# A fused four-layer graph network on one core: GpSimd's work for the first block is put off, the first block's loop over row tiles is reordered, and a small first layer is computed on 96 partitions

## The chip, the cores and the metric

The kernel runs on one core of one Trainium2 chip. The time is the device time of one execution in microseconds (us); before the change it was 3078.63 us, the median of 3 runs (3078.52 to 3081.78).

## What is computed

Four graph layers in a row on 1250 nodes with 512 features and 20000 edges, each added to `x` after a layer norm and a ReLU. The first layer holds nearly all that the change touches:

```python
h = maximum(layernorm(x), 0)
emb  = concat([sin(noise * freqs), cos(noise * freqs)])          # 1250 x 64
cond = silu(emb @ f_w1 + f_b1) @ f_w2 + f_b2                     # 64 -> 16 -> 16
for i in range(4):                                               # four blocks
    y = xhat(h) * (1 + cond @ s1_w[i] + s1_b[i]) + cond @ b1_w[i] + b1_b[i]
    q, k, v = y @ wq[i] + bq[i], y @ wk[i] + bk[i], y @ wv[i] + bv[i]
    att = softmax over the edges that leave each node, 4 heads of 128
    h = h + att_sum(v) @ wo[i] + bo[i]
    y = xhat(h) * (1 + cond @ s2_w[i] + s2_b[i]) + cond @ b2_w[i] + b2_b[i]
    h = h + relu(y @ m_w1[i] + m_b1[i]) @ m_w2[i] + m_b2[i]
x = x + h
# then a mean over neighbours, a gated relational layer and a two-step mean layer
```

`xhat` is the normalised row. The sums over edges are done with dense 1250 x 1250 matrices of edge counts. The mean of the last layer divides by the number of edges that enter each node.

## The kernel before

There is no scheduler: each engine has its own program, in the order in which it is written, and the engines wait for each other by semaphores. Nodes lie as 10 row tiles of 125 (T = 10, P = 125), or transposed on 128 partitions (`yT`).

**Head of the program.** SyncE (SP) loads the edge lists, the conditioning's small weights `fw1`, `fw2`, `fb1`, `fb2` and then `x`, all with no wait (L485 to L490). Semaphore `pre_in` counts the small weights and `x`; VectorE waits for it before it makes the phases (`first_phases`, L806). GpSimd fills constants, and signals `consts_set`, for which VectorE's first operation waits.

**Placement of edges.** 160 steps (EC = 160) follow. In each, GpSimd writes one `row_hot`, VectorE two `slot_hot`, and TensorE multiplies them (L1584) into one PSUM tile. Other work is woven in by step number: the statistics of `x`; at step 10 the first conditioning layer (L1591) with ScalarE's bias and exponential (L1315, L1317); at step 25 VectorE's end of the SiLU (`finish_silu`, L838 to L845: add one, reciprocal, product), on 16 partitions x 1250 elements; at 30, 35 and 40 the second layer (L1596); from 46 on the first norm.

**After the steps.** VectorE makes `placef`, `placei` and the constants `ident_r` (L940 to L963), and then, group by group (59 groups), one-hot matrices from which TensorE builds the counts (L1608, L1615) and ScalarE copies them (L1345, L1348). GpSimd, after its last `row_hot`, goes on at once to block 0: `stack_matrices(1)` (L663 and twice L666, the matrices of the second norm, from `stage`, which shares `oT`), and the bias of the output row, added to all of `x` in one instruction (L690). Both are wanted much later: the first (`cw_ready`) by ScalarE's first `copy_o`, which overwrites `oT`, and by the second norm; the second (`xbias_done`) by VectorE at head 1.

**The loop over row tiles in block 0.** The counts are needed transposed. For each row tile t, TensorE transposes 10 pieces of 125 x 125 (`turn_counts`, L1628) into one PSUM tile, ScalarE copies that to one of three buffers (`copy_turned`, two instructions at L1357), SP writes the buffer to HBM (`crow_d`, L522), VectorE makes a mask from it (`mask_row`, L990), TensorE makes the scores (`max_scores`, L1704), and VectorE takes their masked maximum in two halves (`masked_max`, L1014). `turn_counts(t + 1)` stands ahead of `max_scores(t)` on TensorE, and may write only after ScalarE has copied row tile t. After row tiles 2, 4, 6 and 8 (`TAKE_AT`) TensorE makes one part of head 1's projections (8 matmul records at L1636), which ScalarE takes to `qk_hi` (`high_part`, L1371) and VectorE to `qk_lo` (`low_part`, L1005). ScalarE also sums each row tile of `ct` into `per_in` (L1403, with a throw-away output `junk` in `pacc`). ScalarE's order in it is:

```python
for t in range(T):
    copy_turned(t)
    A.activation(junk, ct[:, t, :], ACT.Copy, accum_out=per_in[:, t:t + 1])
    A.drain()
    if t in TAKE_AT:
        high_part(1, TAKE_AT.index(t))
```

After the loop come the negated maxima (L1020, L1022), `max_row(0)` (L1742), two more parts of projections, and the heads. Each block ends with a two-layer perceptron; its first product is the `up` loop: 12 jobs of 8 matmul records at L1636, each taken over by ScalarE with ReLU (L1434), in two PSUM slots.

## Time and profile before

| what | value |
|---|---|
| median of 3 runs | 3078.63 us (3078.52 to 3081.78) |
| the profiled execution, its own time | 3081.62 us |
| its span, first to last instruction | 3079.9 us |
| TensorE busy | 2855.9 us, 93% |
| VectorE busy | 2052.6 us, 67% |
| ScalarE busy | 866.2 us, 28% |
| GpSimd busy | 714.1 us, 23% |
| mean granted TensorE clock | 0.969 |
| chain that ended last, by engine | PE 73%, DVE 17%, issue 4%, ACT 3% |

PE is TensorE's matmul queue, PEld its weight loads, DVE VectorE, ACT ScalarE, POOL GpSimd. A name with q (ACTq, SPq) is that engine's sequencer. The chain follows the execution back from the last instruction, at each step to what released it. The stages that matter here, in us of the span: placement steps 41 to 200, the constants after them 199 to 220, groups 220 to 388, block 0's first projections 388 to 409, its loop over row tiles 409 to 460, its heads from 472, its `up` loop 787 to 816.

### The profile page before, as it was taken

The page shows a single profiled execution, that of the slowest core. Times are in us where ns is not written, and L with a number is a line of the kernel's source. Part 1 is how long each engine was busy: PE and PEld are TensorE (multiplying, and loading weights), DVE is VectorE, ACT ScalarE, POOL GpSimd, SP SyncE. Part 2 cuts the span into 40 slices and gives each one's busy share as a digit, 9 for nine tenths or more (in the row PEclk, how much of TensorE's full clock was granted, in tenths as well). Part 3 has the DMA queues.
Part 4 walks back from the last instruction along what each step waited for, and adds up shares of the span by engine and source line. Part 5 has one row for each costly group of instructions (what it writes and reads, how often), then busy time and mean ns, then how long its engine had stood idle before and what let it go on. Part 6 is the DMA issues. An engine that isn't in the chain of part 4 may idle for free.

```text
span 3079.9 us, 31253 instructions
## 1 busy us (share of the span) xinstructions
PE 2855.9 (93%) x11230; PEld 1816.5 (59%) x11230; DVE 2052.6 (67%) x3758; ACT 866.2 (28%) x1154; POOL 714.1 (23%) x639
## 2 busy tenths in 40 slices
PE   2869979999999999999999999999999999999999
PEld 0336646676556666555667555667645566556555
DVE  8889946776757776766777674778686876623211
ACT  2218842222212222221222321222322213213221
POOL 3760003333023334031334120334320000000000
PEclk9989989999999999999999999999999999999999
DMA  4000020000400000320000230000145244421001
GB/s 106 1 1 1 1 89 7 1 28 14 126 35 14 1 28 14 97 64 14 1 28 1 66 109 14 1 15 14 47 127 166 65 128 142 130 80 40 14 1 34
DMA packets 74678, 143.61 MB, mean 47 GB/s; under 512 B 11428, under 2 KB 11819, under 8 KB 74524
## 3 DMA queue, kind: packets, MB, share of 16 engines
q1 hardware_dynamic: 68988, 129.58, 13.7%
q0 software_dynamic: 5536, 12.03, 1.2%
q8 instruction: 90, 1.47, 0.2%
q14 instruction: 64, 0.52, 0.1%
HBM read 130.66 MB, written 10.92 MB: 46 GB/s over the span
## 4 chain that ended last, share of the span: by engine, by line
PE 73%; DVE 17%; issue 4%; ACT 3%; DMA 1%; DVEq 1%; POOL 1%; ACTq 0%; SPq 0%
PE ps L1636 13%; PE ps L1859 11%; PE ps L1888 10%; PE ps L1730 6%; PE ps L1833 4%; PE ps L1545 4%; PE ps L1608 4%; DVE prob L1069 4%; DVE x L1059 3%; PE ps L1562 2%; PE ps L1880 2%; PE ps L1719 2%; DVE ps L1014 2%; PE ps L1704 2%; PE ps L1721 2%
## 5 line engine op out<-in xcount | busy, mean ns | idle before, releaser
L706 POOL TENSOR_TENSOR pacc<-pacc,prob 125x628 f32<-125x628 f32 (+1 forms) x288 | 404.7, 1405 | 350.6 <-DVE prob L1088 350.6
L1636 PE MATMUL ps<-yT,w 128*128 128x416 f32 (+1 forms) x1152 | 442.2, 541 | 15.2 <-DVE qk_lo L1005 5.9
L1730 PE MATMUL ps<-prob,big 125*128 125x314 f32 x1280 | 394.8, 431 | 14.0 <-DVE prob L1088 10.9
L1417 ACT ACTIVATE prob<-prob 125x628 f32<-125x628 f32 x320 | 233.0, 728 | 574.7 <-DVE prob L1069 574.7
L1888 PE MATMUL ps<-pieces,counts_r 125*125 125x512 f32 x1400 | 353.3, 406 | 0.0
L1636 PEld LDWEIGHTS ps<-yT,w 128*128 128x128 f32 x1152 | 229.3, 201 | 202.8 <-issue 188.9
L1088 DVE SCALAR_TENSOR_TENSOR prob<-prob,typed 125x628 f32<-125x628 f32 x320 | 260.1, 813 | 70.3 <-ACT prob L1417 68.1
L1888 PEld LDWEIGHTS ps<-pieces,counts_r 125*125 125x125 f32 x1400 | 257.2, 185 | 76.9 <-issue 17.4
L1719 PE MATMUL ps<-qk_hi 128*125 128x314 f32 x640 | 271.5, 424 | 11.2 <-DVE prob L1069 10.6
L1730 PEld LDWEIGHTS ps<-prob,big 125*128 125x128 f32 x1280 | 228.0, 190 | 81.3 <-DVE prob L1088 27.2
L1014 DVE CUSTOM_DVE_ANT_0 ps<-ps,typed 125x628 f32<-125x628 f32 x320 | 257.9, 816 | 10.0 <-PE ps L1704 9.9
L1069 DVE TENSOR_TENSOR prob<-ps,shift 125x628 f32<-125x628 f32 x320 | 257.4, 804 | 6.2 <-PE ps L1721 5.6
L1005 DVE SCALAR_TENSOR_TENSOR qk_lo<-ps,bcol,qk_hi 128x416 fp32r<-128x416 f32 (+1 forms) x96 | 62.3, 651 | 261.5 <-ACT qk_hi L1371 261.5
L702 POOL TENSOR_TENSOR pacc<-prob,zcol 125x628 f32<-125x628 f32 (+1 forms) x32 | 39.3, 1228 | 751.6 <-DVE prob L1088 751.6
L1720 PE MATMUL ps<-qk_lo,qk_hi 128*125 128x314 f32 x640 | 197.9, 309 | 0.0
L1721 PE MATMUL ps<-qk_hi,qk_lo 128*125 128x314 f32 x640 | 197.9, 309 | 0.0
L643 POOL TENSOR_TENSOR rstd<-var,mhalf 125x1 f32<-125x1 f32 x110 | 71.8, 652 | 535.9 <-DVE var L867 535.9
L1115 DVE SCALAR_TENSOR_TENSOR lite_acc<-lite_ring,att_w,lite_acc 128x512 f32<-128x512 f32 x232 | 180.7, 820 | 10.9 <-DMA lite_ring<-in_basis 1.9
L1169 DVE SCALAR_TENSOR_TENSOR w<-basis,att_w,w 128x512 f32<-128x512 f32 x232 | 167.3, 748 | 22.8 <-DMA basis<-in_basis 10.0
L1778 PE MATMUL ps<-w,oT 128*125 128x512 f32 x320 | 180.1, 648 | 1.5 <-DVE x L1059 1.5
L1719 PEld LDWEIGHTS ps<-qk_hi 128*125 128x125 f32 x640 | 120.0, 188 | 103.3 <-DVE prob L1069 82.5
L1371 ACT ACTIVATE qk_hi<-ps,bcol 128x416 fp32r<-128x416 f32 (+1 forms) x96 | 58.1, 609 | 396.6 <-PE ps L1636 396.6
(214 smaller groups left out, 4488.2 us busy)
## 6 DMA issues: line engine op xcount, KB each, us to landing
basis<-in_basis SPq DMA_DIRECT2D x160, 256.0 KB, 2.7
lite_ring<-in_basis SPq DMA_DIRECT2D x120, 256.0 KB, 2.6
w<-in_m_w SPq DMA_DIRECT2D x8, 1024.0 KB, 6.6
w<-in_wk SPq DMA_DIRECT2D x5, 1024.0 KB, 6.4
w<-in_wv SPq DMA_DIRECT2D x4, 1024.0 KB, 5.5
oT<-in_cw SPq DMA_DIRECT2D x8, 512.0 KB, 4.1
w<-in_wq SPq DMA_DIRECT2D x4, 1024.0 KB, 5.4
w<-in_wo SPq DMA_DIRECT2D x4, 1024.0 KB, 5.4
```

Of the source, the lines that this page charges most:

```text
L706: nc.gpsimd.tensor_tensor(pacc[:, c0:c0 + nn], pacc[:, c0:c0 + nn], prob[:, n % 3, p0:p0 + nn], ALU.add).then_inc(psum_done, 1)
L1014: V.tensor_tensor_reduce(out=score_ps(s.slot), in0=score_ps(s.slot), in1=in_quarters(mneg[:, t, c0:c0 + HALF]), scale=1.0, scalar=-BIG, op ...
L1069: V.tensor_tensor(in_quarters(prob[:, n % 3, :]), score_ps(s.slot), in_quarters(shift[:, c0:c0 + HALF]), ALU.add).then_inc(shifted, 1)
L1088: V.scalar_tensor_tensor(out=prob[:, n % 3, 0:nn], in0=prob[:, n % 3, 0:nn], scalar=BIG, in1=ct[:, t, c0:c0 + nn], op0=ALU.min, op1=ALU.mu ...
L1417: A.activation(prob[:, n % 3, :], prob[:, n % 3, :], ACT.Exp, scale=DH ** -0.5).then_inc(exp_done, 1)
L1636: last = mm(lin_ps(job, 128, nn), weight[:, k, m * 128:(m + 1) * 128], lhs[:, k, c0:c0 + nn], start=(k == 0), stop=(k == KD - 1))
L1719: mm(o, hi[:, 1, rows], hi[:, 0, cols], start=True, stop=False)
L1720: mm(o, hi[:, 1, rows], lo[:, 0, cols], start=False, stop=False)
L1721: last = mm(o, lo[:, 1, rows], hi[:, 0, cols], start=False, stop=True)
L1730: last = mm(o_halves[:, b, :], vrow[:, t, h * DH:(h + 1) * DH], prob[:, n % 3, b * QUARTER:(b + 1) * QUARTER], start=(t == 0), stop=(t == ...
L1859: last = mm(post_ps(job, P, D), lhs[:, k, t * P:(t + 1) * P], weight[:, k, :], start=(k == 0), stop=(k == KD - 1))
L1888: last = mm(post_ps(job, P, D), counts_r[:, slot, k, :], pieces[:, piece, k, :], start=(self_ is None and k == 0 and piece == 0), stop=(k ...
```

## The change

1. **GpSimd** in block 0 waits for `mneg_ready` 1 (the mask of row tile 0) ahead of `stack_matrices(1)`, and adds the bias one row tile at a time, piece t after mask t: ten instructions of 512 elements in place of one of 5120.
2. **The loop** takes each part of head 1's projections one row tile later on ScalarE and VectorE (`t - 1 in TAKE_AT`). TensorE's order is as before.
3. **The sums** `per_in` go from ScalarE's loop to the `up` loop of block 0, one after each of its first ten jobs, with `junk` in `shift`. VectorE's maximum and reciprocal of them go to block 1.
4. **Conditioning**: the first layer's product writes 96 partitions from a weight with three copies of `f_w1` at columns 0, 32 and 64; ScalarE takes from each of the three column ranges of 418 its own 32 partitions, so that `z`, `zexp` and `silu` are 96 x 418 in place of 16 x 1250. SP loads `fw1`, `fw2` and `fb1` three times, after `consts_set`; GpSimd clears `fw1` and `fb1` ahead of it.

```diff
...
         ident16 = sk("ident16", [P, P], F16)
-        fw1 = sk("fw1", [2 * FREQS, COND], F32)
-        fw2 = sk("fw2", [COND, 128], F32)
-        fb1 = sk("fb1", [COND, 1], F32)
+        fw2 = sk("fw2", [96, 128], F32)
+        fb1 = sk("fb1", [96, 1], F32)
         fb2 = sk("fb2", [128, 1], F32)
...
         emb = yT[0:2 * FREQS, 3, :]
-        z = hidT[0:COND, 0, :]
-        zexp = hidT[0:COND, 1, :]
-        silu = hidT[0:COND, 2, :]
+        z = hidT[0:96, 0, 0:418]
+        zexp = hidT[0:96, 1, 0:418]
+        silu = hidT[0:96, 2, 0:418]
 
...
         egr = sa("egr", [128, BUCKETS], F32)
+        fw1 = sa("fw1", [2 * FREQS, 96], F32)
         gcmp = sa("gcmp", [128, GROUPS + 1, BUCKETS], F32)
...
         skip_x_last = prob[:].rearrange("p s n -> p (s n)")[:, 2 * D:3 * D]
-        junk = pacc[:].bitcast(F16)[:, 0:N]
         cw = sl("cw", [128, 4, D], F32R)
...
         shift = sl("shift", [P, N], F32)
+        junk = shift[:].bitcast(F16)[:, 0:N]
         bias_r = sl("bias_r", [P, D], F32R)
...
             sp.dma_start(noise, a["node_vec1"].partition_broadcast(2 * FREQS)).then_inc(phase_ready, 16)
-            for dst_, name in ((fw1, "L0_gnn_f_w1"), (fw2, "fw2_stack"), (fb1, "f_b1"), (fb2, "fb2_stack")):
-                sp.dma_start(dst_[:], a[name]).then_inc(pre_in, 16)
+            sp.wait_ge(consts_set, 1)
+            for k in range(3):
+                for dst_, name in ((fw1[:, 32 * k:32 * k + COND], "L0_gnn_f_w1"), (fw2[32 * k:32 * k + COND, :], "fw2_stack"),
+                                   (fb1[32 * k:32 * k + COND, :], "f_b1")):
+                    sp.dma_start(dst_, a[name]).then_inc(pre_in, 16)
+            sp.dma_start(fb2[:], a["fb2_stack"]).then_inc(pre_in, 16)
             sp.dma_start(x[:], a["x"].rearrange("(t p) d -> p t d", p=P)).then_inc(pre_in, 16)
...
             nc.gpsimd.memset(ident[:], 0.0)
+            nc.gpsimd.memset(fw1[:], 0.0)
+            nc.gpsimd.memset(fb1[:], 0.0)
             nc.gpsimd.memset(ident16[:], 0.0)
...
                     if half == 0:
+                        if i == 0:
+                            pool.wait_ge(mneg_ready, 1)
                         stack_matrices(1, at(i, 32, 32))
...
                     pool.wait_ge(blkc_in, at(i, 32, 32))
-                    nc.gpsimd.tensor_tensor(x[:], x[:], brow[:, 1:2, :].to_broadcast([P, T, D]),
-                                            ALU.add).then_inc(xbias_done, 1)
+                    if i:
+                        nc.gpsimd.tensor_tensor(x[:], x[:], brow[:, 1:2, :].to_broadcast([P, T, D]),
+                                                ALU.add).then_inc(xbias_done, 1)
+                    else:
+                        for t in range(T):
+                            pool.wait_ge(mneg_ready, t + 1)
+                            last = nc.gpsimd.tensor_tensor(x[:, t, :], x[:, t, :], brow[:, 1, :], ALU.add)
+                        last.then_inc(xbias_done, 1)
                     for h in range(HEADS):
...
                 dve.wait_ge(phase_ready, 16)
-                dve.wait_ge(pre_in, 80)
+                dve.wait_ge(pre_in, 176)
                 V.tensor_scalar(turns, noise, freq[:], 1.0 / 16.0, ALU.mult, ALU.mult)
...
                     masked_max(0, 2 * t + 1)
-                    if i == 0 and t in TAKE_AT:
-                        low_part(1, TAKE_AT.index(t))
+                    if i == 0 and t - 1 in TAKE_AT:
+                        low_part(1, TAKE_AT.index(t - 1))
                 negate_max(0)
...
                 if i == 0:
-                    dve.wait_ge(edges_counted, 2)
                     V.tensor_tensor(per_out, per_out, edges_out[:, :, 1], ALU.add)
-                    V.tensor_scalar(per_in[:], per_in[:], 1.0, None, ALU.max)
                     V.drain()
                     V.reciprocal(per_out, per_out)
+                if i == 1:
+                    dve.wait_ge(edges_counted, T)
+                    V.tensor_scalar(per_in[:], per_in[:], 1.0, None, ALU.max)
+                    V.drain()
                     V.reciprocal(per_in[:], per_in[:])
...
             A.activation(cw[:, 0:2, :], stage, ACT.Copy).then_inc(cw_hi, 1)
-            for (c0, nn), job in zip(COLS, hj):
+            for k, job in enumerate(hj):
+                rows = slice(32 * k, 32 * k + 32)
                 act.wait_ge(lin_full, job.full)
-                A.activation(z[:, c0:c0 + nn], lin_ps(job, COND, nn), ACT.Identity, bias=fb1[:]).then_inc(lin_empty[job.slot], 1)
+                A.activation(z[rows, :], lin_ps(job, 96, 418)[rows, :], ACT.Identity, bias=fb1[rows, :]).then_inc(lin_empty[job.slot], 1)
             A.drain()
...
                         copy_turned(t)
-                        A.activation(junk, ct[:, t, :], ACT.Copy, accum_out=per_in[:, t:t + 1])
-                        A.drain()
-                        if t in TAKE_AT:
-                            high_part(1, TAKE_AT.index(t))
-                    A.drain().then_inc(edges_counted, 2)
+                        if t - 1 in TAKE_AT:
+                            high_part(1, TAKE_AT.index(t - 1))
                 else:
...
                                  bias=bcol[:, 2, k:k + 1]).then_inc(lin_empty[job.slot], 1)
+                    if i == 0 and n < T:
+                        A.activation(junk, ct[:, n, :], ACT.Copy, accum_out=per_in[:, n:n + 1])
+                        A.drain().then_inc(edges_counted, 1)
                     if n == 5 and i + 1 < BLOCKS:
...
                 if c == HIDDEN_AT:
-                    pe.wait_ge(pre_in, 80)
+                    pe.wait_ge(pre_in, 176)
                     pe.wait_ge(emb_ready, 2)
-                    for (c0, nn), job in zip(COLS, hj):
+                    for k, job in enumerate(hj):
                         reuse(job)
-                        mm(lin_ps(job, COND, nn), fw1[:], emb[:, c0:c0 + nn], start=True, stop=True).then_inc(lin_full, 1)
+                        mm(lin_ps(job, 96, 418), fw1[:], emb[:, 416 * k:416 * k + 418], start=True, stop=True).then_inc(lin_full, 1)
                 if c in COND_AT:
                     pe.wait_ge(silu_ready, 1)
-                    (c0, nn), job = COLS[COND_AT.index(c)], cj[COND_AT.index(c)]
+                    k = COND_AT.index(c)
+                    (c0, nn), job, rows = COLS[k], cj[k], slice(32 * k, 32 * k + COND)
                     reuse(job)
-                    mm(lin_ps(job, 128, nn), fw2[:], silu[:, c0:c0 + nn], start=True, stop=True).then_inc(lin_full, 1)
+                    mm(lin_ps(job, 128, nn), fw2[rows, :], silu[rows, c0 - 416 * k:c0 - 416 * k + nn],
+                       start=True, stop=True).then_inc(lin_full, 1)
                 n, rest = divmod(c - NORM_AT, NORM_EVERY)
```

GpSimd's program from the last `row_hot` to block 0's first sum of probabilities, before and then now:

```order
L648 TENSOR_SCALAR row_hot<-col_iota,slot_row 125x128 x38
L663 TENSOR_TENSOR cw<-oT,zcol 128x1024
L666 TENSOR_TENSOR cw<-oT,cw 32x1024 x2
L690 TENSOR_TENSOR x<-x,brow 125x5120
L702 TENSOR_TENSOR pacc<-prob,zcol 125x628
```

```order
L654 TENSOR_SCALAR row_hot<-col_iota,slot_row 125x128 x38
L669 TENSOR_TENSOR cw<-oT,zcol 128x1024
L672 TENSOR_TENSOR cw<-oT,cw 32x1024 x2
L704 TENSOR_TENSOR x<-x,brow 125x512 x10
L716 TENSOR_TENSOR pacc<-prob,zcol 125x628
```

The order of the instructions stays; the new wait stands between the first row and the second, and the one bias instruction has become ten.

ScalarE in block 0's loop, from the second half of row tile 2's copy on (`prob` is the buffer of the transposed counts, `typed` is `ct`), before and then now:

```order
L1357 ACTIVATE prob,edges_out<-ps 125x250
L1403 ACTIVATE pacc,per_in<-typed 125x1250
L1371 ACTIVATE qk_hi<-ps,bcol 128x418
L1357 ACTIVATE prob,edges_out<-ps 125x1000
L1357 ACTIVATE prob,edges_out<-ps 125x250
L1403 ACTIVATE pacc,per_in<-typed 125x1250
L1357 ACTIVATE prob,edges_out<-ps 125x1000
L1357 ACTIVATE prob,edges_out<-ps 125x250
L1403 ACTIVATE pacc,per_in<-typed 125x1250
L1371 ACTIVATE qk_hi<-ps,bcol 128x416
L1357 ACTIVATE prob,edges_out<-ps 125x1000
```

```order
L1374 ACTIVATE prob,edges_out<-ps 125x250
L1374 ACTIVATE prob,edges_out<-ps 125x1000
L1374 ACTIVATE prob,edges_out<-ps 125x250
L1388 ACTIVATE qk_hi<-ps,bcol 128x418
L1374 ACTIVATE prob,edges_out<-ps 125x1000
L1374 ACTIVATE prob,edges_out<-ps 125x250
L1374 ACTIVATE prob,edges_out<-ps 125x1000
L1374 ACTIVATE prob,edges_out<-ps 125x250
L1388 ACTIVATE qk_hi<-ps,bcol 128x416
L1374 ACTIVATE prob,edges_out<-ps 125x1000
```

The sums are gone from between the copies, and the part whose product follows row tile 4 (the second `qk_hi` row) is taken after the copy of row tile 5, no longer ahead of it.

## Rows read from the trace of the kernel before

**Rows 1.** The profile's page, busy time of the engines

```profile
PE 2855.9 (93%) x11230; PEld 1816.5 (59%) x11230; DVE 2052.6 (67%) x3758; ACT 866.2 (28%) x1154; POOL 714.1 (23%) x639
```

**Rows 2.** Timeline of VectorE, 66 to 79 us (start, length, engine, line, operation, idle before)

```profile
67.70 0.79 DVE L840 TENSOR_SCALAR big<-big 16x1250 f32<-16x1250 f32 x1
68.57 7.95 DVE L842 RECIPROCAL big<-big 16x1250 f32<-16x1250 f32 x1
76.59 1.45 DVE L844 TENSOR_TENSOR big<-big 16x1250 f32<-16x1250 f32 x1
```

**Rows 3.** Timeline of TensorE, 66 to 110 us

```profile
78.91 2.71 PE L1584 MATMUL ps<-slot_hot,row_hot 125*128 125x472 f16 x5 [10.43 <-DVE slot_hot L923]
```

**Rows 4.** Timeline of VectorE, 199 to 220 us

```profile
202.46 0.25 DVE L945 TENSOR_SCALAR bk<-bk 128x60 f32<-128x60 f32 x1
...
202.91 2.33 DVE L948 TENSOR_SCALAR placef<-bk 128x59 f32<-128x59 f32 x1
...
205.61 2.18 DVE L953 CAST placei<-placef 128x59 int32<-128x59 f32 x1
...
208.90 10.19 DVE L961 CAST ident_r<-ident 125x125 fp32r<-125x125 f32 x1
```

**Rows 5.** Timeline of GpSimd, 199 to 220 us

```profile
199.38 3.27 POOL L663 TENSOR_TENSOR cw<-oT,zcol 128x1024 fp32r<-128x1024 f32 x1 [0.16 <-issue]
202.79 4.94 POOL L666 TENSOR_TENSOR cw<-oT,cw 32x1024 fp32r<-32x1024 f32 x2
208.05 10.96 POOL L690 TENSOR_TENSOR x<-x,brow 125x5120 f32<-125x5120 f32 x1 [0.31 <-issue]
```

**Rows 6.** Timeline of TensorE, 176 to 232 us

```profile
220.85 5.92 PE L1608 MATMUL ps<-onehot_src,onehot_dst 128*125 128x512 f16 x24 [20.76 <-DVE onehot_src L979]
```

**Rows 7.** Timeline of ScalarE, 386 to 500 us

```profile
423.50 1.00 ACT L1357 ACTIVATE prob<-ps 125x1000 f16<-125x1000 f16 x1 [2.10 <-DMA crow_d<-prob]
...
434.08 0.61 ACT L1371 ACTIVATE qk_hi<-ps,bcol 128x416 fp32r<-128x416 f32 x1 [5.08 <-PE ps L1636]
```

**Rows 8.** Chain that ended last, 425 to 460 us (start, length, what)

```profile
441.39 3.33 PE ps L1636 x8
...
444.99 1.26 ACTq L1404
...
446.70 1.23 ACT pacc L1403 x2
...
449.57 1.33 PE ps L1628 x10
450.90 1.15 PE ps L1704 x4
...
457.20 0.49 DVE typed L990
...
457.82 0.82 DVE ps L1014
```

**Rows 9.** Timeline of TensorE, 432 to 472 us

```profile
436.09 0.80 PE L1628 MATMUL ps<-ident,typed 125*125 125x125 f16 x10 [2.04 <-ACT prob L1357]
436.69 0.82 PE L1704 MATMUL ps<-qk_hi 128*125 128x314 f32 x4
...
460.07 2.46 PE L1742 MATMUL ps<-ident_r,nmx 125*125 125x126 f32 x10 [4.32 <-DVEq L1023]
462.68 7.59 PE L1636 MATMUL ps<-yT,w 128*128 128x416 f32 x16 [0.16 <-ACT shift L1382]
```

**Rows 10.** Windows by 4 us (length; PE, PEld, DVE, ACT, POOL busy; PEclk, DMA share, GB/s)

```profile
460.00:464.00 4.00, 3.77 (x12) 3.09 (x13) 0.00 (x0) 1.49 (x3) 0.00 (x0) 0.50 0.72 240
```

**Rows 11.** Windows by 1 us, the load of x and of the first weights

```profile
32.00:33.00 1.00, 0.00 (x0) 0.00 (x0) 1.00 (x1) 0.00 (x0) 0.00 (x0) 1.00 0.01 4
```

**Rows 12.** Timeline of the SP queue, 0 to 42 us

```profile
4.74 0.33 SPq L490 DMA_DIRECT2D x<-in_x  x1
```

**Rows 13.** Groups of TensorE, 786 to 817 us (busy, mean ns; idle before)

```profile
L1636 PE MATMUL ps<-yT,w 128*128 128x416 f32 (+1 forms) x80 | 28.2, 513 | 1.3 <-ACT big L1434 1.3
```

2 lines of the change are left out of this document (1 added, 1 removed).

## The prediction, made blind

> **What bounds the kernel now.** I read the page first. TensorE is busy 93% of the span [rows 1], so only its gaps, and matmuls that ran at the lower of its two clocks, can be won, and those lie mostly in the first 480 us. I then followed the chain that ended last through that part and read each engine's timeline where the chain leaves TensorE. There are three such places.
>
> First, VectorE's end of the SiLU takes 0.79, 7.95 and 1.45 us [rows 2], of which the reciprocal is nearly all. TensorE stands idle for 10.43 us and goes on when VectorE has made the next `slot_hot` [rows 3].
>
> Second, after the placement steps a small cast to int32 takes 2.18 us, and the cast of a 125 x 125 tile 10.19 us, where an operation of the same kind on 60 elements takes 0.25 [rows 4]. GpSimd's instructions explain it: `placef` begins at 202.91, just after GpSimd's `cw` instruction at 202.79, and ends at 205.24, the middle of the two that make up 4.94 us; `placei` ends at 207.79, and the pair at 207.73; the cast of `ident` ends at 219.09, and GpSimd's addition to `x` at 219.01 [rows 4, 5]. Three times VectorE is let go when a GpSimd instruction ends. TensorE waits 20.76 us in all here [rows 6].
>
> Third, block 0's loop over row tiles. ScalarE first waits for a transfer of `crow_d`, until 423.50 [rows 7]. From then on a pair of row tiles takes 10.66 us (441.39 to 452.05, the end of row 450.90). In it the chain goes from TensorE's product (3.33) to ScalarE, which has waited for the product (5.08 us idle [rows 7]) and only then copies a row tile (1.26 and what follows), sums (1.23), copies the next, and then back to TensorE's transposes (1.33) and scores (1.15) [rows 8].
>
> **The change, term by term.**
>
> *SiLU.* The three operations go from 1250 to 418 elements in a partition, 832 fewer. A fixed part of 0.15 us each taken off, an element costs 6.24 ns in the reciprocal, 0.51 and 1.04 in the others [rows 2]. That is 5.19 + 0.43 + 0.87 = **6.5 us**, all on VectorE and in TensorE's gap of 10.43 us [rows 3]. No row shows these operations on 96 partitions. The mask, with the same 1250 elements (of two bytes) on 125 partitions, takes 0.49 us [rows 8] where 16 partitions took 0.79, so the time goes by elements in a partition; the other bound, nothing won, I leave to the range's upper part with the loads. GpSimd is ahead at that point. The matmuls, with 96 output partitions in place of 16, stay as many and as wide.
>
> *Loads.* SP now waits for `consts_set`, some 5 us into the span, and issues six more small loads. `x` was issued at 4.74 [rows 12]; with those issues of 0.45 to 0.65 us each I put it at about 10.7, 5.9 us later. The queue was quiet by 32.0 [rows 11], with the first weights behind `x` in it, so `x` lands by about 35 to 37. VectorE asks for it at 36.2. I cost this at nothing; what hides it is the head's long VectorE operations, and each us beyond costs one. Bound: 3 us. GpSimd's two more memsets come before VectorE's first input is there.
>
> *GpSimd put off.* `placef` falls by 2.08, `placei` by 1.93 to 1.98 and the cast of `ident`, with 125 elements, by about 9.95 [rows 4]: **14.0 us** at the start of the groups, which no other engine holds: TensorE waits for VectorE alone there [rows 6]. Bounds 13.5 and, if TensorE also starts at a better clock after a shorter rest, 15.
>
> Where does the work go? In the loop, mask 0 ends at about 409.8 and GpSimd then runs 3.27 + 4.94 us [rows 5] to 418.2, and the pieces for row tiles 0, 1 and 2, some 1.1 to 1.3 us each (10.96 for ten [rows 5]), to about 422. Masks 1 and 2 may wait up to 1.2 us for an instruction of GpSimd's to end, but nothing is late before ScalarE's wait for the transfer ends at 423.50 [rows 7]. That wait is the cover. After it each piece begins when its mask is written and the next mask comes 2.7 us or more later. So I cost it at 0; without the cover it would be 8.2 us for the matrices. Queued behind the new wait on GpSimd are only these and the sums of probabilities, wanted at 474.
>
> The Trainium skill (SBUF — State Buffer, section "Who interferes with whom") says that a VectorE instruction in a 2-port mode and a GpSimd instruction exclude each other for the whole length of whichever came first. The trace agrees three times over, as above. It also speaks against the new place, since the mask is of such a kind; by it the cost could be as the second rival says.
>
> *The loop.* ScalarE no longer holds row tile 5, 7 or 9 back for the product, and doesn't sum. The cycle of a pair becomes TensorE's: product, transposes, copy, transposes, scores. At full clock that is 2.82 (28.2 us for 80 records, 8 to a product [rows 13]) + 0.80 [rows 9] + 1.55 (a copy: two instructions of which the first takes 1.00 [rows 7], with its gaps) + 0.80 + 0.82 [rows 9] = 6.8 us. At the clock of this trace's slower records it is 3.33 + 0.80 + 1.55 + 1.33 + 1.15 = 8.2 [rows 8]. TensorE now rests less than the 2.04 us of before [rows 9], after which it was still fast, so I take 7.3. The product after row tile 4 ends at about 434.1, when ScalarE takes it [rows 7]. Two more pairs end at 448.7; then come the scores of row tile 9, two maxima of 0.82 [rows 8], the part taken later (0.65) and the negation: `max_row` at about 452.0, where it was at 460.07 [rows 9]. **8.1 us**, with bounds 5 and 9.5. The transfers of `crow_d` don't bind: ScalarE waited for one of ten.
>
> *Behind it.* `max_row` and the 16 records of projection ran 2.46 and 7.59 us [rows 9], at half clock at first [rows 10]; 16 records at full clock take 5.6 [rows 13]. TensorE's rest ahead of them falls from 4.32 us [rows 9] to about 2.6. I take **1.0 us** of the 2.2, and **0.2** for two small operations on VectorE that leave. Bounds 0 and 2.4.
>
> *Sums in the `up` loop.* Ten times some 1.5 us (the chain's 1.23 and the accumulator's read [rows 8]) beside 0.6 of ReLU make 2.2 us of ScalarE in a product's 2.82 [rows 13]. Hidden under TensorE, cost 0; at most 1.6 us, at the job where ScalarE also converts the next block's matrices.
>
> Sum: 6.5 + 14.0 + 8.1 + 1.0 + 0.2 = 29.8 us. The profiled execution took 3081.6, so it would take 3051.8; it was 3.0 above the median of the runs. Against the median of 3078.63 I predict **3048.8 us**.
>
> **Rivals.** (1) *The loop hardly gains* (0.14): TensorE stays at its slower clock, or each `crow_d` transfer takes as long as the first did (over 14 us from its issue at about 409.2), and ScalarE waits again. For it: the first wait exists. Against: no second one does. The other terms are left, 20.5 us: 3058.1. (2) *GpSimd's work lands on the loop* (0.05): masks wait for it and the transfer's wait doesn't cover. The matrices cost 8.2 us and each of seven later masks up to 1.1: 15.9 us back, 3064.7. Against: the times above. (3) *The long casts are not GpSimd's doing* (0.04): then 14.0 us stay, 3062.8. Against it are three ends within 0.1 us of each other. (4) *Slower* (0.02): ScalarE's sums throttle the `up` loop. Its two PSUM slots empty only when ScalarE is through, so the loop's pace becomes ScalarE's as soon as a sum takes over 2.2 us (2.82 less 0.6); ten of 5.2 us each would give back all 29.8, and ten of 6 us 37.8, which makes 3086.6. The row of 1.23 us speaks against it. (5) *`x` comes late* (0.05), by more than 3 us: at 5 us, 3053.8.
>
> **How the numbers follow.** The forecast has 0.70. All its low ends (3.5 for SiLU and loads, 13.5, 5, 0) make 22.0 us, 3056.6; its high ones (6.5, 15, 9.5, 2.4) make 33.4, 3045.2. The range reaches to rival 1 above and 1 us beyond below, for the scatter of the median: 3044.2 to 3058.5. What a measurement of this kernel can tell from no change is about 0.2%, 6.2 us. All cases but the fourth are faster by more than that: faster 0.96, same 0.02 (several of the ends together), slower 0.02.
>
> **What would show it.** Right: a reciprocal of 2.7 to 2.8 us on 96 partitions and TensorE's gap there near 4; the cast of `ident` below 0.4 us, and the first group's matmul some 20.5 us earlier (200.3); GpSimd's `cw` instructions after mask 0 and over before ScalarE's wait for the transfer ends; a pair of row tiles of 7 to 8 us; no wait of TensorE for ScalarE in the `up` loop of block 0 beyond the 1.3 us of now [rows 13]. Wrong: a wait of VectorE at 36 us for `x`; more than one wait for `crow_d`; masks that take over 1 us behind the first three; a total that differs from the sum of these places, which would mean that a stage further on had used the gap.

## The result, and the profile after

| what | before | changed |
|---|---|---|
| median | 3078.57 us (3076.79 to 3081.78, 4 runs) | 3041.79 us (3041.54 to 3042.7, 4 runs) |
| ratio | | 0.988, 95% interval 0.9863 to 0.9897 |
| profiled execution, span | 3081.62 us, 3079.9 us | 3042.7 us, 3041.0 us |
| PE, DVE, ACT, POOL busy | 2855.9, 2052.6, 866.2, 714.1 us | 2845.3, 2034.2, 865.5, 714.3 us |
| mean granted TensorE clock | 0.969 | 0.975 |

The kernel is 36.8 us faster. The forecast was 29.8, and the median lies 2.4 us below the low end of its range. Two later sets of runs gave 35.3 and 32.8 us (3078.49 to 3043.16, 3076.5 to 3043.72): the median of before moved between 3076.5 and 3079.9 from set to set, that of the changed kernel between 3041.8 and 3043.7. So the forecast was short by 3 to 7 us.

The page's first rows after, to [rows 1]:

```profile
span 3041.0 us, 31271 instructions
...
PE 2845.3 (94%) x11230; PEld 1808.7 (59%) x11230; DVE 2034.2 (67%) x3758; ACT 865.5 (28%) x1154; POOL 714.3 (23%) x650
```

**Start.** Timeline of VectorE, 35 to 71 us (start, length, engine, line, operation, shapes; idle time before in brackets), to [rows 2]:

```profile
35.76 0.93 DVE L823 TENSOR_SCALAR yT<-yT,freq 64x1250 f32<-64x1250 f32 x1
...
67.37 0.36 DVE L854 TENSOR_SCALAR big<-big 96x418 f32<-96x418 f32 x1
67.81 2.76 DVE L856 RECIPROCAL big<-big 96x418 f32<-96x418 f32 x1
70.64 0.59 DVE L858 TENSOR_TENSOR big<-big 96x418 f32<-96x418 f32 x1
```

The reciprocal takes 2.76 us (7.95 before), the other two 0.36 and 0.59 (0.79 and 1.45). At 35.76 no wait stands before VectorE's first operation that needs the loads behind `x`'s place in the queue, and none came later: the loads cost nothing. TensorE's gap there, to [rows 3]:

```profile
72.10 2.71 PE L1601 MATMUL ps<-slot_hot,row_hot 125*128 125x472 f16 x5 [3.95 <-DVE slot_hot L937]
```

3.95 us in place of 10.43. **Constants.** VectorE from 196 to 198 us, to [rows 4], and TensorE at the start of the groups, to [rows 6]:

```profile
196.04 0.18 DVE L962 TENSOR_SCALAR placef<-bk 128x59 f32<-128x59 f32 x1
...
196.60 0.19 DVE L967 CAST placei<-placef 128x59 int32<-128x59 f32 x1
...
197.91 0.23 DVE L975 CAST ident_r<-ident 125x125 fp32r<-125x125 f32 x1
```

```profile
199.89 6.49 PE L1627 MATMUL ps<-onehot_src,onehot_dst 128*125 128x512 f16 x20 [6.62 <-DVE onehot_src L993]
```

The cast of `ident` takes 0.23 us where it took 10.19, TensorE's idle time is 6.62 where it was 20.76, and the first group's matmul starts at 199.89 (220.85 before; 200.3 was forecast). **Where GpSimd's work went.** Timelines of GpSimd and of VectorE's masks, 390 to 404 us, to [rows 5]:

```profile
390.35 1.89 POOL L669 TENSOR_TENSOR cw<-oT,zcol 128x1024 fp32r<-128x1024 f32 x1 [197.94 <-DVE typed L1004]
392.38 4.91 POOL L672 TENSOR_TENSOR cw<-oT,cw 32x1024 fp32r<-32x1024 f32 x2
397.62 3.71 POOL L704 TENSOR_TENSOR x<-x,brow 125x512 f32<-125x512 f32 x3 [0.33 <-issue]
403.99 1.28 POOL L704 TENSOR_TENSOR x<-x,brow 125x512 f32<-125x512 f32 x1 [2.66 <-DVE typed L1004]
```

```profile
389.77 0.49 DVE L1004 TENSOR_SCALAR typed<-prob 125x1250 bf16<-125x1250 f16 x1 [0.56 <-issue]
...
392.47 2.61 DVE L1004 TENSOR_SCALAR typed<-prob 125x1250 bf16<-125x1250 f16 x1
...
396.72 0.92 DVE L1004 TENSOR_SCALAR typed<-prob 125x1250 bf16<-125x1250 f16 x1
...
403.42 0.49 DVE L1004 TENSOR_SCALAR typed<-prob 125x1250 bf16<-125x1250 f16 x1 [4.01 <-ACT prob L1374]
```

Mask 1 is held for 2.1 us (its instruction is recorded as 2.61 us long where a free one takes 0.49), mask 2 for 0.4, later ones not at all; and ScalarE still waits before the fourth row tile, 7.52 us here, so this costs nothing at mask 3. **The loop.** A pair is two row tiles, from one product of TensorE (L1655) to the next. Chain that ended last, 413 to 426 us (start, length, what), to [rows 8], and TensorE's `max_row`, to [rows 9]:

```profile
413.84 2.79 PE ps L1655 x8
416.63 0.60 PE ps L1647 x10
...
418.15 0.56 ACT prob L1374 x3
418.72 0.04 issue
418.76 0.79 PE ps L1647 x10
419.55 0.63 PE ps L1723 x4
420.18 2.81 PE ps L1655 x8
```

```profile
426.06 1.09 PE L1761 MATMUL ps<-ident_r,nmx 125*125 125x126 f32 x8 [2.50 <-DVEq L1037]
...
427.86 7.22 PE L1655 MATMUL ps<-yT,w 128*128 128x416 f32 x16
```

ScalarE stands in the chain only with the copy (416.63 + 0.60 to 418.76), the product and its sum are gone from it, and a pair of row tiles takes 6.34 us (413.84 to 420.18) in place of 10.66. `max_row` is 34.0 us earlier than before.

**Where the gain is.** Two profiles of before and three of the changed kernel (the first, and those of r1_before, r2_after and r4_after below) give, as means:

| stretch | before | changed | gain | forecast |
|---|---|---|---|---|
| start to mask 0 | 409.90 | 389.94 | 20.0 | 20.5 |
| mask 0 to `max_row` | 48.80 | 36.95 | 11.8 | 8.1 |
| `max_row` to the first exponential | 13.49 | 11.76 | 1.7 | 1.2 |
| first exponential to the end of the span | 2605.8 | 2602.6 | 3.2 | 0 |

### The profile page after: what moved, and what is told of

It reads as the page before. It is cut to its first block, busy times and chain, and to the rows that moved or that the text cites. A ratio compares the mean times of both kernels' runs of the same rounds, so it can differ in the third digit from the quotient of the medians.

```text
span 3041.0 us, 31271 instructions
## 1 busy us (share of the span) xinstructions
PE 2845.3 (94%) x11230; PEld 1808.7 (59%) x11230; DVE 2034.2 (67%) x3758; ACT 865.5 (28%) x1154; POOL 714.3 (23%) x650
## 4 chain that ended last, share of the span: by engine, by line
PE 73%; DVE 16%; issue 4%; ACT 3%; DMA 1%; DVEq 1%; POOL 1%; SPq 0%; ACTq 0%
PE ps L1655 13%; PE ps L1878 11%; PE ps L1907 10%; PE ps L1749 6%; PE ps L1852 5%; PE ps L1562 5%; PE ps L1627 4%; DVE prob L1085 4%; DVE x L1075 3%; PE ps L1579 2%; PE ps L1899 2%; PE ps L1738 2%; DVE ps L1028 2%; PE ps L1723 2%; ACT prob L1431 2%
## 5 line engine op out<-in xcount | busy, mean ns | idle before, releaser
L1655 PE MATMUL ps<-yT,w 128*128 128x416 f32 (+1 forms) x1152 | 440.8, 540 | 15.0 <-DVE qk_lo L1019 5.9
L1655 PEld LDWEIGHTS ps<-yT,w 128*128 128x128 f32 x1152 | 228.7, 201 | 201.3 <-issue 187.7
L1738 PE MATMUL ps<-qk_hi 128*125 128x314 f32 x640 | 271.7, 424 | 11.6 <-DVE prob L1085 11.3
L1131 DVE SCALAR_TENSOR_TENSOR lite_acc<-lite_ring,att_w,lite_acc 128x512 f32<-128x512 f32 x232 | 180.4, 819 | 11.5 <-DMA lite_ring<-in_basis 1.9
L1723 PE MATMUL ps<-qk_hi 128*125 128x314 f32 x640 | 152.9, 330 | 7.8 <-issue 6.8
```

The lines of the kernel that those rows point to most:

```text
L1655: last = mm(lin_ps(job, 128, nn), weight[:, k, m * 128:(m + 1) * 128], lhs[:, k, c0:c0 + nn], start=(k == 0), stop=(k == KD - 1))
L1723: last = mm(score_ps(s.slot)[:, b, :], qk_hi[:, h % 2, 0, t * P:(t + 1) * P], qk_hi[:, h % 2, 1, c0:c0 + QUARTER], start=True, stop=True)
L1738: mm(o, hi[:, 1, rows], hi[:, 0, cols], start=True, stop=False)
```

## The experiments

All are timed against the kernel before, which ran again in each set of runs; a ratio is taken to before in the same set, with its 95% interval, and a gain to the set's median of before. The table has, for each profile, the stretch from mask 0 to mask 3 (it holds ScalarE's wait for the `crow_d` transfer), and that from mask 3 to `max_row`, worked out from the starts of VectorE's masks and of TensorE's `max_row`.

| kernel | median us | mask 0 to 3 | mask 3 to `max_row` | sum |
|---|---|---|---|---|
| before, first profile | 3078.57 | 15.69 | 35.08 | 50.77 |
| r1_before: again | 3078.14 | 14.32 | 32.51 | 46.83 |
| e1_cond96: before + 96 partitions | 3073.33 | 14.30 | 34.15 | 48.45 |
| e2_pool: before + GpSimd's put-off | 3062.30 | 15.39 | 34.95 | 50.34 |
| e4_sums: before + sums moved | 3076.81 | 13.25 | 34.24 | 47.49 |
| e13_split_before: before + stores in two | 3077.50 | 11.71 | 35.48 | 47.19 |
| e3_order: before + order | 3065.02 | 13.78 | 26.03 | 39.81 |
| e5_loop: before + order + sums | 3066.30 | 14.92 | 25.69 | 40.61 |
| changed, first profile | 3041.79 | 13.65 | 22.64 | 36.29 |
| r2_after: again | 3043.16 | 13.73 | 24.75 | 38.48 |
| r4_after: again | 3043.72 | 13.48 | 22.61 | 36.09 |
| e10_sums_back: changed, sums in the loop | 3047.11 | 14.85 | 25.51 | 40.36 |
| e6_no_pool: changed, GpSimd as before | 3057.65 | 13.87 | 24.33 | 38.20 |
| e9_fill: e6_no_pool + a product twice | 3060.07 | 15.37 | 25.00 | 40.37 |
| e7_pool5: changed, matrices at mask 4 | 3046.00 | 13.55 | 25.70 | 39.25 |
| e12_early: changed, matrices at the groups' end | 3045.19 | 15.08 | 24.99 | 40.07 |
| e8_split: changed, stores in two | 3038.71 | 9.50 | 24.54 | 34.04 |
| e14_early_sums_back: e11 with sums in the loop | 3042.14 | 9.08 | 24.61 | 33.69 |
| e11_split_early: e8 + e12 | 3036.89 | 7.37 | 23.66 | 31.03 |
| r3_best: e11 again | 3036.23 | 8.15 | 23.69 | 31.84 |

### The four parts one by one

**e1_cond96.** The hunks of the diff on `fw1`, `fb1`, `fw2`, `z` and their loads, and nothing else.

> The kernel before with the conditioning's first layer on 96 partitions and nothing else (loads, matmuls, SiLU). Theory: the reciprocal falls from 7.95 us to 2.8, the other two of VectorE by 1.3 in all, and all of it reaches the end: the last placement step, the groups and block 0 stand 6.3 to 6.8 us earlier, and the time is 3072 us. Rival: the placement steps behind the SiLU are held by GpSimd's or TensorE's pace and take it back: VectorE's first copy of a typed bucket stands less than 3 us earlier, time 3076 to 3079. Second rival: what is won at 70 us depends on the other parts.

3073.33 us, ratio 0.9981 (0.9972 to 0.9991): 6.6 us less than the set's 3079.91, by the interval 2.8 to 8.6. The reciprocal took 2.76 us. In the trace mask 0 stands 5.3 us and the first exponential 7.3 us earlier. The term holds by itself.

**e2_pool.** The two hunks on GpSimd alone: `pool.wait_ge(mneg_ready, 1)`, and ten pieces of the bias.

> The kernel before with GpSimd's put-off alone (matrices wait for mask 0, the bias addition in ten pieces), the loop and the sums as before. Theory: the casts to placei and of ident fall to about 0.25 us, 14 us at the start of the groups, 1.2 of it given back by the first group's matmuls at the lower clock; the loop stays at its old pace (a pair of row tiles 10.66 us) because its order is the old one; time 3065.5. Rival A: the put-off work is what made the new loop fast beyond the forecast (shorter wait for the crow_d transfer, TensorE at the upper clock after it): then mask 3 follows mask 0 by 13.7 us and not 15.7, and a pair takes under 10 us; time about 3060. Rival B: in the old loop GpSimd's pieces hold masks back and a pair takes over 11 us; time above 3068.

3062.3 us, ratio 0.9946 (0.9929 to 0.9962), 17.6 us less than the set's before. In the trace mask 0 is 13.5 us earlier and the first exponential 13.6; the other 4 stand behind the first exponential (2600.8 us against 2606.9), where the edit touches nothing. The loop took 50.34 us, in the range of kernels with its order, and mask 3 followed mask 0 by 15.4. Pairs took 9.1 to 11.6 us, as they did in r1_before (9.1 to 11.5) with no work of GpSimd beside them: rival A is out, and so is B.

**e3_order.** On the kernel before:

```diff
-                    if i == 0 and t in TAKE_AT:
-                        low_part(1, TAKE_AT.index(t))
+                    if i == 0 and t - 1 in TAKE_AT:
+                        low_part(1, TAKE_AT.index(t - 1))
```

and the same for ScalarE's `high_part`, the sum left ahead of it.

> The kernel before with ScalarE and VectorE taking each product of the loop one row tile later, the sums left in the loop, GpSimd's work and the SiLU as before. Theory (the order lets TensorE go on, and TensorE that rests less keeps the upper clock): transposes at 0.80 and scores at 0.82 us behind the first wait, a pair of row tiles at ScalarE's own pace, 2 x (1.55 copy + 1.45 sum) + 0.65 product and gaps = about 7.0 us against 10.66; max_row about 10 us earlier against mask 3. Time 3067. Rival (the sums are what holds the pair): the pair stays above 9 us, time 3074 or more.

3065.02 us, ratio 0.9948 (0.9932 to 0.9965), 14.9 us less. The loop takes 39.81 us against 46.8 to 50.8, and the last two pairs 6.34 us (437.81 to 444.15 at the masks), below what I expected. I had taken 7.0 us for ScalarE's own work, but it does its two copies, two sums and the take in 6.1 us and waits 0.26 us for the product in each pair; the chain there has neither sum. The pairs before those ran at the lower clock and took 10.0 and 8.6 us (masks 4 to 6 and 5 to 7). The expectation of TensorE's clock behind the first wait was half right: transposes at 0.79 us, then 1.33.

**e4_sums.** On the kernel before, the sum taken out of the loop and put into the `up` loop, the takes where they were.

> The kernel before with the ten sums moved to the up loop alone, the loop's old order, GpSimd's work and the SiLU as before. Theory: the chain product, ScalarE's take, copy, transposes, copy stays, without two sums of 1.45 us: a pair takes 7.8 us against 10.66, or 7.3 if TensorE also keeps the upper clock; max_row 7 to 9 us earlier against mask 3; nothing lost in the up loop of block 0 (under 0.3 us). Time 3070. Rival (only the order matters): pair above 9.5 us, time 3075. Second rival: the sums cost in the up loop, which grows by 1 us or more.

3076.81 us, ratio 0.999 (0.998 to 1.0), 3.1 us less, at the edge of what can be told from nothing. The expectation of 7.8 us for a pair was wrong: it took 10.2 (435.70 to 445.91 at the masks). Timeline of its ScalarE around a product:

```profile
437.81 0.20 ACT L1359 ACTIVATION_READ_ACCUMULATOR prob<-ps 125x1 f32 x1
443.93 0.61 ACT L1373 ACTIVATE qk_hi<-ps,bcol 128x416 fp32r<-128x416 f32 x1 [5.92 <-PE ps L1638]
444.43 1.00 ACT L1359 ACTIVATE prob<-ps 125x1000 f16<-125x1000 f16 x1
```

Without the sum, ScalarE waits 5.92 us for the product where it waited 5.08 [rows 7]. The old order put the copy behind the product's end, and a sum there fell mostly into the wait. The `up` loop of block 0 did not grow: one window over it, length, busy time of PE, PEld, DVE, ACT and POOL, granted clock, DMA share and GB/s, of before and of the changed kernel:

```profile
787.00:816.00 29.00, 28.20 (x80) 15.02 (x80) 22.44 (x32) 7.54 (x13) 0.00 (x0) 1.00 0.44 127
```

```profile
751.70:780.70 29.00, 28.20 (x80) 15.02 (x80) 21.13 (x30) 19.88 (x33) 0.00 (x0) 1.00 0.42 118
```

ScalarE has 19.9 us of work in place of 7.5 and TensorE's 28.20 us stay. Rival 4 of the forecast, the slower side, is out: a sum took 1.24 + 0.19 us.

### Do the parts add, and does GpSimd have a hand in the loop?

**e5_loop** is e3_order and e4_sums together on the kernel before; **e6_no_pool** is the changed kernel with both GpSimd hunks undone.

> The kernel before with the loop's new order and the sums moved, GpSimd's work and the SiLU as before. From mask 0 to max_row the kernel before took 50.8 us, the changed one 36.3, the order alone 39.8, the sums alone 47.5. Theory (order and fewer sums, with TensorE's clock following from how little it rests; GpSimd's put-off work has no part in it): 36 to 38 us here too, pairs of 6.34, time 3065. Rival (GpSimd's work and the later mask behind it shortened the first part): 39 us or more, time 3068.

> The changed kernel with GpSimd's matrices and bias at their old place. Theory: the casts take 10 us and 2 again, the first group's matmul is 14.1 us later and no other stage changes: 36 to 38 us from mask 0 to max_row; time 3055 to 3057. Rival: the put-off also gave the loop 2 to 3 us (then 39 us in the loop and a time of 3058 or more), or its pieces cost the loop something (under 35.5 us in the loop, time 3054).

e5_loop: 3066.3 us, ratio 0.9956 (0.994 to 0.9973), 11.3 us less than its set's before, loop 40.61. The parts add: 6.6 (e1_cond96), 17.6 (e2_pool) and 11.3 make 35.5 us, and the changed kernel was 32.8 to 36.8 us faster. The order alone had gained 14.9 in its set, so on the kernel before the sums show no gain on top of it. e6_no_pool: 3057.65 us, ratio 0.9934 (0.9917 to 0.995), loop 38.20, TensorE idle for 21.67 us before the groups. The same loop code thus took 40.61 and 38.20 us with GpSimd out of it, and 36.29 in the changed kernel. In e6_no_pool TensorE rested long before the fourth row tile and ran slower behind it. Timeline of its transposes, and of those of the changed kernel:

```profile
418.38 1.33 PE L1639 MATMUL ps<-ident,typed 125*125 125x125 f16 x10 [4.97 <-ACT prob L1366]
```

```profile
403.44 0.80 PE L1647 MATMUL ps<-ident,typed 125*125 125x125 f16 x10 [1.72 <-ACT prob L1374]
```

That suggested that GpSimd's held masks helped: they push the third row tile's scores and the product behind them later, into the wait, so that TensorE rests less. Three runs went after it.

**e7_pool5** (`mneg_ready` 5 in place of 1), **e12_early** (`pool.wait_ge(bucket_placed, GROUPS)` in its place) and **e9_fill** (on e6_no_pool, ahead of the loop's first product):

```diff
+                            if n == 0:
+                                job = g["proj"][1][0]
+                                c0, nn = COLS[0]
+                                reuse(job)
+                                for k in range(KD):
+                                    mm(lin_ps(job, 128, nn), w[1][:, k, 128:256], yT[:, k, c0:c0 + nn],
+                                       start=(k == 0), stop=(k == KD - 1))
                             col_product(g["proj"][1][n], yT, n % 3, w[1 + n // 3], 1)
```

> The changed kernel with GpSimd's matrices put off to mask 4 and not mask 0, so that the two long instructions and five pieces of the bias in a row run after ScalarE's wait for the transfer, beside a running loop. Theory (a mask and a GpSimd instruction exclude each other, and only the wait for the transfer hid that): one to three masks behind mask 4 take 1 to 3 us in place of 0.48, and mask 0 to max_row takes 38 to 40 us against 36.3; time 3044 to 3046. Rival (the loop has slack for it, no cover is needed): masks are held but max_row is not later by over 0.5 us; time 3042.

> The run without GpSimd's put-off (e6_no_pool) with the loop's first product (row tile 2) computed twice, into the same place and with the same result: 2.8 us more work for TensorE just before it waits for row tile 4, in a wait that ends with ScalarE's transfer in any case. Without it TensorE rested about 4.6 us there and ran the next transposes in 1.33 us and the scores at the lower clock, 24.3 us from mask 3 to max_row; in the changed kernel, where held masks had pushed that product later, it rested 1.72 us, the transposes took 0.80, and it was 22.6 us. Theory (the length of TensorE's rest before the fourth row tile sets the clock after it, and the held masks shortened it by chance): transposes 0.80 and 22.5 to 23.2 us from mask 3 to max_row; the time falls by 1 to 1.5 us against e6_no_pool (3057.65), to 3056.4, though work was added. Rival (the clock there has another cause): 24.3 us, time 3057.6 or more.

> The changed kernel (stores in one transfer) with GpSimd's matrices at the end of the groups in place of after mask 0. Theory: no mask is held, but ScalarE's wait for the transfer hides that, so mask 3 stays where it was (403 to 404); TensorE now rests 4.6 us before it and has the lower clock behind it, so that max_row is 1.5 to 3 us later than in the changed kernel: time 3043 to 3044, slower for having less contention. Rival (the held masks cost something after all): time 3041 or less.

e7_pool5: 3046.0 us, ratio 0.9892 (0.9875 to 0.9908), loop 39.25. The rows of GpSimd and of the masks:

```profile
408.14 1.89 POOL L669 TENSOR_TENSOR cw<-oT,zcol 128x1024 fp32r<-128x1024 f32 x1 [215.51 <-DVE typed L1004]
410.18 4.91 POOL L672 TENSOR_TENSOR cw<-oT,cw 32x1024 fp32r<-32x1024 f32 x2
415.42 13.41 POOL L704 TENSOR_TENSOR x<-x,brow 125x512 f32<-125x512 f32 x10 [0.33 <-issue]
```

```profile
409.89 0.49 DVE L1004 TENSOR_SCALAR typed<-prob 125x1250 bf16<-125x1250 f16 x1
...
417.55 1.06 DVE L1004 TENSOR_SCALAR typed<-prob 125x1250 bf16<-125x1250 f16 x1
...
421.79 0.77 DVE L1004 TENSOR_SCALAR typed<-prob 125x1250 bf16<-125x1250 f16 x1
...
424.20 1.06 DVE L1004 TENSOR_SCALAR typed<-prob 125x1250 bf16<-125x1250 f16 x1
```

The long instructions fell between two masks (the mask at 409.89 is over before the pair at 410.18 begins, the next comes at 415.44), and only the pieces held masks, by 0.3 to 0.6 us. The last of them counts: TensorE waits 3.52 us before `max_row` where it waited 2.50. So 1.0 us is the held mask. r2_after, the changed kernel with the same slow transposes behind the wait (1.30 us there, 1.33 here), took 24.75 us from mask 3 to `max_row`, 0.95 less than this run; the rest of the 3 us over the changed kernel's first profile goes with the clock.

e12_early: 3045.19 us, ratio 0.9889 (0.9872 to 0.9905). No mask was held, and the loop took 40.07 us, as expected longer; but TensorE ran its transposes at 0.79 us behind the wait (rest 3.82) and at 1.33 before it and after it, so not for the reason I gave. e9_fill: 3060.07 us, ratio 0.9938 (0.9922 to 0.9955), a miss: the rest fell to 2.88 us, the first transposes took 0.80, the next ones, 2.6 us later, 1.33, and mask 3 to `max_row` took 25.0 (24.33 without the fill). The length of the rest just before is not what sets the clock alone: behind 3.82 us (e12_early) the transposes took 0.79, behind 3.24 us (r2_after) 1.30. The medians of the changed kernel (3041.8, 3043.2, 3043.7) lie below that of e12_early, but the ratios' intervals overlap. Whether held masks help is open.

### The wait for the transfer

**e8_split** and, on the kernel before, **e13_split_before**. Waits on these semaphores count to 32 in place of 16:

```diff
-                sp.dma_start(crow_d[s * P:(s + 1) * P, :], turned_counts(s)).then_inc(crow_out[s % 3], 16)
+                for p0, p1 in ((0, 112), (112, P)):
+                    sp.dma_start(crow_d[s * P + p0:s * P + p1, :], turned_counts(s)[p0:p1, :]).then_inc(crow_out[s % 3], 16)
```

and the same for `ct2_d`.

> The changed kernel with each store of the typed and of the turned counts in two transfers, of 112 partitions and of 13, where it was one of 125 (whose engines were busy for 0.32 of their time in the stretch of the stores while it moved 115 GB/s). Theory: a transfer of 125 partitions keeps 5 of 16 DMA engines busy, so that the stores stand in a queue until ScalarE's wait; on 112 partitions all sixteen work, the queue is empty when the first crow_d store is issued, ScalarE's 7.5 us of idle time before its fourth row tile go, and mask 3 follows mask 0 by 8 to 10 us in place of 13.65; time 3037. Then GpSimd's matrices run without cover, and up to 2.5 us of it may come back at masks 1 to 3: time up to 3039. Rival: the rate is set by memory or by the queue and not by the engines: DMA share and wait stay, time 3042.

> The kernel before with each store in two transfers (112 and 13 partitions), nothing else. Theory: ScalarE's wait goes here too; mask 3 follows mask 0 by 9 to 11 us (its first product is still taken first) in place of 15.7; time 3074 to 3076. Rival: the wait was hidden by the old order's own chain; time 3078 or more.

e8_split: 3038.71 us, ratio 0.9869 (0.9853 to 0.9885); mask 3 follows mask 0 by 9.50 us and mask 2 by 2.55, so the wait is gone. Now the held masks count: GpSimd's matrices keep mask 1 for 2.61 us with no wait behind it to hide that. e13_split_before: 3077.5 us, ratio 0.9996 (0.9986 to 1.0005), mask 0 to 3 in 11.71 us where it took 14.3 to 15.7, and no gain to be measured, as its rival had it. The wait was worth 2.6 to 4.0 us locally, and in the old order little of that arrived.

**e11_split_early** has both, the split stores and the matrices at the groups' end; **e14_early_sums_back** is that with ScalarE's sums back in the loop.

> e8_split (stores in two transfers each) with GpSimd's matrices at the end of the groups (all buckets placed) and not after mask 0, where VectorE has about 10.8 us without work; the bias stays in ten pieces behind the masks. Theory: no mask is held (mask 1 0.49 us and not 2.61), mask 3 follows mask 0 by 7.0 to 7.5 us and not 9.5, time 3036.5. Rival: GpSimd's matrices now hold VectorE's additions of the typed counts (1.52 us for two) and TensorE's first products wait: mask 0 is later than 389.8 by as much as was won.

> The fastest version so far (e11_split_early) with ScalarE's sums back in the loop behind the copies. Theory (a sum delays the copy behind it only where no product lies beside it, and then TensorE's rests grow and its clock falls): mask 0 to max_row 33 to 35 us against 31.0, time 3039 to 3041. Rival (the order alone does it, a sum lies beside the product): 31.0 to 31.7 us, time 3037.

e11_split_early: 3036.89 us, ratio 0.9862 (0.9846 to 0.9879). Mask 3 follows mask 0 by 7.37 us and the loop takes 31.03. Windows of the changed kernel and of this one over the stores (columns as above), 370 to 376 us and 384 to 390:

```profile
370.00:376.00 6.00, 6.00 (x15) 3.18 (x14) 2.04 (x3) 0.61 (x1) 0.00 (x0) 0.78 0.32 110
...
384.00:390.00 6.00, 3.93 (x23) 2.33 (x22) 4.01 (x7) 3.08 (x7) 0.00 (x0) 1.00 0.32 118
```

```profile
370.00:376.00 6.00, 6.00 (x15) 3.11 (x15) 1.99 (x3) 0.61 (x1) 5.09 (x3) 0.82 0.96 302
...
384.00:390.00 6.00, 3.93 (x22) 2.33 (x21) 4.00 (x7) 3.08 (x7) 0.00 (x0) 1.00 0.00 0
```

The DMA engines' share rises from 0.32 to 0.96 and the rate from 110 to 302 GB/s, and when the first `crow_d` store is issued (389.7) the queue is empty, where the one-piece stores still moved 118 GB/s. 0.32 is near 5/16. The Trainium skill (DMA: Bandwidth & Descriptors, section "Why a DMA increments its semaphore by 16 and not by 1") says that a transfer runs on the largest number of engines up to 16 that divides its outermost dimension on both sides. Worked out from that rule, it is 5 for 125 partitions and 16 for 112. The two windows agree. A split into two other sizes was not run, so that it is the size 112, and not the cutting in two, is not separated here. GpSimd's matrices ran from 368.5 to 375.4. VectorE had no work until 374.01, and after it the matrices held one pair of its additions (L1000), which took 2.18 us from 374.58 where the next pairs took 1.52. Nothing of these 0.66 us arrived: mask 0 still came at 389.83 (389.69 in e8_split, 388.56 in r3_best): the expectation's rival is out.

e14_early_sums_back: 3042.14 us, ratio 0.988 (0.9862 to 0.9898), loop 33.69. Its four runs (3041.8 to 3045.6) and the eight of e11 and r3_best (3034.9 to 3038.4) do not meet. The loop is 1.9 to 2.7 us longer with the sums, 0.9 to 1.7 of it before mask 3, where no product lies beside them, and the stretch from `max_row` to the first exponential is 1.1 to 1.3 us longer (13.04 against 11.98 and 11.73). The rest of the 5.3 to 5.9 us between the medians is not placed. Likewise e10_sums_back:

> The changed kernel with ScalarE's ten sums back in the loop, behind the copies, and the takes still one row tile later. On the kernel before, the order alone gave a pair of 6.34 us with the sums in it. Theory (with the new order a sum lies beside TensorE's product and costs nothing): pairs of 6.34 us, 36 to 37.5 us from mask 0 to max_row, time 3042 to 3043. Rival (the sums bind once the rest is fast): pairs of 7 us and more, time 3044 or above.

3047.11 us, ratio 0.9894 (0.9877 to 0.991), the loop 40.36. Its last two pairs took 6.34 us, so the sums do not bind there; the loss is before (transposes of 1.33 us already at the second row tile, after a rest of 1.26 in place of 0.92).

### How much is scatter

> The kernel before, unchanged, for a second profile. Theory (part of the 14.5 us is scatter): mask 0 to max_row takes 48 to 50 us here against 50.77 in the first profile, with mask 3 13.3 to 15.5 us behind mask 0. Rival (its first profile is typical): 50.8 again within 0.5.

> The changed kernel, unchanged, for a second profile. Theory (its loop had luck with the clock and the wait): mask 0 to max_row takes 37 to 40 us against 36.29, and the median is 1 us or more above 3041.8. Rival (it is typical: masks held by GpSimd always shorten TensorE's rest): 36.3 within 0.7, and a median of 3041.5 to 3042.5.

r1_before: 3078.14 us, ratio 0.9996 (0.9986 to 1.0006), loop 46.83, 3.9 us shorter than in the first profile of the same kernel. r2_after: 3043.16 us, ratio 0.9875 (0.9858 to 0.9893), loop 38.48, 2.2 longer than in its first. The clock can be seen in TensorE's timeline and in a window (columns as above) behind the wait, r2_after first and then r4_after, one kernel with the same instructions:

```profile
404.20 1.30 PE L1647 MATMUL ps<-ident,typed 125*125 125x125 f16 x10 [3.24 <-ACT prob L1374]
```

```profile
404.00:409.00 5.00, 4.41 (x27) 4.02 (x28) 3.04 (x7) 2.70 (x8) 1.48 (x2) 0.53 0.29 95
```

```profile
403.08 0.80 PE L1647 MATMUL ps<-ident,typed 125*125 125x125 f16 x10 [1.62 <-ACT prob L1374]
```

```profile
403.00:408.00 5.00, 3.76 (x31) 3.02 (x32) 4.09 (x10) 3.24 (x10) 2.38 (x2) 1.00 0.30 99
```

The granted clock is 0.53 (almost all of it at 1.2 GHz) in the one and 1.00 (2.4 GHz) in the other. In r2_after the slow stretch began earlier, with the second row tile (transposes of 1.21 and 1.13 us, 0.76 and 0.80 in the other).

> e11_split_early again, beside the changed kernel in one set. Theory: mask 0 to max_row 31 to 33 us, median 3036 to 3038, 4 to 6 us below the changed kernel's. From the first exponential to the end 2600 to 2607 us, one of the values seen before. Rival (its first result was luck): within 2 us of the changed kernel.

> The changed kernel for a third profile and in one set with the version above. Theory: mask 0 to max_row between 36.3 and 40 us, median 3041.5 to 3043.5; from the first exponential to the end 2600 to 2604 us. Rival: below 3040, then the version above gains less than thought.

In one set: r3_best 3036.23 us, ratio 0.9861 (0.9845 to 0.9878), loop 31.84; r4_after 3043.72 us, ratio 0.9885 (0.9869 to 0.9902), loop 36.09. The version with the split stores and the early matrices is 7.5 us faster than the changed kernel there, 4.9 by the medians of the first sets. From the first exponential to the end the twenty profiles took between 2600.1 (e1_cond96) and 2607.2 us (e10_sums_back), e3_order 2603.9, e5_loop and e6_no_pool 2600.6, with no relation to the edit that I can see. Two profiles of one kernel differed there by 2.2 to 2.7 us (before and r1_before; the changed kernel and r2_after; e11_split_early and r3_best).

## Why the prediction fell short

**SiLU, 6.5 us: right.** e1_cond96 gave 6.6, and TensorE's gap fell by 6.48 (10.43 to 3.95). The row of the reciprocal (2.76) is what the count of elements gave. **Loads, 0: right.** No wait stood at 35.76. **GpSimd put off, 14.0: right.** TensorE's idle time before the groups fell by 14.14 us, and e6_no_pool, which undoes it, is 13.9 to 15.9 us slower than the changed kernel's medians. About 0.7 us of the 20.7 was given back before mask 0, in groups that start at a lower clock (20 matmuls in 6.49 us, where before 24 took 5.92 [rows 6]; the granted clock of the first 6 us is 0.54, and 0.75 before); I had left that term out and had even allowed a gain for it. The cover was named rightly: the matrices and the first pieces lay before ScalarE's wait ended, and e8_split shows what they cost without it. Only the sizes differed: mask 1 was held 1.4 to 2.1 us in the three profiles, not 1.2.

**The loop, 8.1 us with bounds 5 and 9.5: this step failed.** The mechanism was right (the cycle of a pair became TensorE's), but the term was too small: the loop gave 14.5 us in the first pair of traces and 11.8 in the means. Cut at ScalarE's copy of row tile 3, where its wait ends, and at its takes of the second and the fourth product of the loop, the traces read as follows (us; the forecast's base is the first profile of before).

| stretch | before, two profiles | changed, three profiles | gain in means | forecast |
|---|---|---|---|---|
| mask 0 to the copy of row tile 3 | 14.20, 12.84 | 12.17, 12.24, 11.99 | 1.4 | 0 |
| to the second take | 10.58, 8.57 | 8.39, 10.50, 8.37 | 0.5 | 0 |
| two pairs, to the fourth take | 21.13, 20.57 | 12.69, 12.70, 12.70 | 8.2 | 6.5 |
| to `max_row` | 4.86, 4.85 | 3.04, 3.04, 3.03 | 1.8 | 1.6 |

The step that was wrong is "TensorE now rests less than the 2.04 us of before, after which it was still fast, so I take 7.3". A pair took 6.35 us: the two pairs took 12.7 us in all fourteen runs with the new order, with and without the sums, and 20.4 to 22.2 in the six with the old one. Two things were in the 7.3. The full-clock sum of 6.8 was too large by 0.5, since records of pipelined matmuls overlap: in the chain the transposes count 0.60 and 0.79 and the scores 0.63, not 0.80, 0.80 and 0.82. And I went halfway to the slow clock, while TensorE rests 0.91 us in such a pair and none of these pairs was slow. That is 1.9 us of the forecast's 14.6.

The second row of the table, which the forecast left as it was, follows TensorE's clock and not the order. Of the fifteen runs that still wait for the transfer, it took 8.4 to 8.6 us in the four with a granted clock of 1.00 there (two of the old order, r1_before and e1_cond96, and two profiles of the changed kernel), and 10.1 to 11.8 in the eleven with 0.56 to 0.71, of both orders. So part of what is beyond the forecast is luck: in the first pair of traces this row gave 2.2 us and the wait, which ended later in the first profile of before than in its second, gave 2.0. What decides the clock there is open.

That the order does it and not the sums, I had not separated. The four profiles with the old loop (before, r1_before, e1_cond96, e2_pool) have a mean of 49.1 us, the two with the new order and the sums still in it (e3_order, e10_sums_back) 40.1: the order gives 9.0. The sums give 1.6 alone (e4_sums) and 1.9 to 2.7 where the wait is gone, both within what one kernel's profiles differ by, and nothing in the two pairs. The medians with them back in the loop are 3.4 to 5.9 us higher (e10_sums_back, e14_early_sums_back), so moving them is worth something, but where is in part open. **Behind the loop, 1.2:** 1.7 in the means. TensorE's projection took 7.22 us with 2.50 of rest ahead of `max_row`, so the lower clock stayed for its first part.

**Behind the first exponential, 0:** 3.2 us in the means and 3.6 in the first traces, though the only edits there add work: ten sums to the `up` loop, which did not grow, and two small operations of VectorE to block 1. I put this down to chance, in where the lower clock falls, and not to a term, but it is not shown: both profiles of before were at the upper end of twenty (2606.9, 2604.7), and in the 200 us stretches that begin 400 and 600 us behind the first exponential the granted clock of before fell to 0.95 (873 to 1073 us in the first profile, 1071 to 1271 in the second), where the three profiles of the changed kernel have 0.96 and 0.97. The forecast took the difference of one profile to the median (3.0 us) as its only scatter, and its range ended 1 us below its lowest sum. That was too narrow: one kernel's profiles differ by 2 to 4 us in the loop and by 2 to 3 behind it, and the medians of before by 3.4 from set to set.

**Rivals.** 1 (the loop hardly gains), 2 (GpSimd's work lands on the loop), 3 (the casts), 4 (slower) and 5 (`x` late) did not come about. Rival 2 is real in another kernel: without the wait (e8_split) mask 1 stays held and mask 3 is 1.4 to 2.1 us later than with the matrices moved (e11_split_early, r3_best). The Trainium skill's rule (SBUF — State Buffer, "Who interferes with whom"), by which a VectorE instruction in a 2-port mode and one of GpSimd exclude each other for a whole instruction, is borne out by mask 1's 2.61 us beside the matrices and 0.48 us without them.

## What to carry to other kernels

When an engine is freed in a loop, read the new cycle from the chain of waits and not from the sum of records, and try its order before its work: here one row tile's delay in taking a product gave 9 us in the loop, and moving ten sums 1.6 to 2.7. Put work of GpSimd that excludes VectorE where VectorE has nothing to do; behind a wait it is hidden only as long as the wait is there. And look at the DMA share of a queue in a stretch: a steady 0.32 with 125 partitions left two thirds of the DMA engines' time unused, and a split of 112 and 13 emptied the queue.

## What was not expected of the hardware

- Stores of 125 partitions ran at 110 to 118 GB/s with the DMA engines busy for 0.32, and the same bytes as 112 and 13 partitions at 302 GB/s and 0.96.
- TensorE's clock in a stretch differs between profiles of one kernel: the transposes behind the same wait took 0.80 us at a granted clock of 1.00 and 1.30 at 0.53, and a rest of 2.88 us was followed by 0.80 us first and by 1.33 us 2.6 us later (e9_fill). Nor did the shorter rest always get the upper clock: transposes took 1.30 us behind a rest of 3.24 (r2_after) and 0.79 behind one of 3.82 (e12_early).
- The end of ScalarE's wait varied with no edit near it: mask 3 came 34.6 to 37.1 us after the first store in the fifteen traces with stores of one piece.
